# Global attention: the product with the values in two halves of 256 columns, one behind the score matmuls of each head

## The reference

```
xn = layernorm(x)
q, k, v = split(xn @ w_qkv.T)        # 16 heads of 16, q and k rotated (rope)
scores = einsum('blhd,bmhd->bhlm', q, k) / 4
attn = softmax(scores)
s = einsum('bhlm,bmhd->blhd', attn, v) @ w_out.T
```

## Time and profile before

| | us |
|---|---|
| median of 3 runs | 2440.17 (2438.77 to 2447.61) |
| the profiled execution | 2444.06 |
| its span, first to last instruction | 2442.3 |
| global attention within it | about 190 to 888 |

### The profile page before, as it was taken

The page is one execution under the profiler, slowest core; times in us unless marked ns, Lnnn a source line. Parts: engine busy times, 40 slices in busy tenths (PEclk is TensorE's granted clock), DMA queues, the critical chain, the costliest instruction groups (busy, mean ns, idle before and its releaser), DMA issues. The chain is left out here.

```text
span 2442.3 us, 40512 instructions
## 1 busy us (share of the span) xinstructions
PE 2274.1 (93%) x12576; PEld 1315.1 (54%) x12576; DVE 1623.6 (66%) x3777; ACT 1371.3 (56%) x2570; POOL 597.0 (24%) x482
## 2 busy tenths in 40 slices
PE   7969999999999978999999999899999999999868
PEld 4533333333333336666666667567567666666534
DVE  5678999999999926565665556556556556556326
ACT  2216777777777756565555456456456546556321
POOL 4411200000000025333233333233233233323000
PEclk9968999999999989999999999999999999999989
DMA  4584212211112010000000000000100000000016
GB/s 144 182 249 132 57 43 60 61 52 55 50 52 61 27 46 1 1 1 1 0 0 0 0 0 26 1 1 9 35 1 1 0 0 0 0 0 0 1 35 186
DMA packets 71891, 95.83 MB, mean 39 GB/s; under 512 B 13884, under 2 KB 49168, under 8 KB 71696
## 3 DMA queue, kind: packets, MB, share of 16 engines
q1 hardware_dynamic: 71808, 94.78, 12.9%
HBM read 60.67 MB, written 39.49 MB: 41 GB/s over the span
## 5 line engine op out<-in xcount | busy, mean ns | idle before, releaser
L655 DVE TENSOR_REDUCE maxima<-ps_m 128x1 f32<-128x512 f32 x1024 | 635.2, 684 | 63.5 <-PE ps_m L546 59.5
L718 ACT ACTIVATE probs<-ps_st 128x1024 f32<-128x1024 f32 x512 | 496.1, 1021 | 173.1 <-PE ps_st L578 171.5
L546 PE MATMUL ps_m<-k_st,q_st 48*128 48x512 f32 x1024 | 390.7, 468 | 31.8 <-DVE k_st L682 16.2
L1246 ACT ACTIVATE l_probs<-l_probs,l_neg_max 128x256 f32<-128x256 f32 x512 | 254.1, 497 | 222.4 <-DVE l_neg_max L1375 222.4
L578 PE MATMUL ps_st<-q_st,k_st 50*128 50x512 f32 x1024 | 306.5, 426 | 2.7 <-DMA q_st<-max_rows 1.6
L1375 DVE CUSTOM_DVE_ANT_1 l_probs<-ring,l_mask 128x256 f32<-128x256 f32 x384 | 140.1, 421 | 226.9 <-PE ring L1072 226.4
L578 PEld LDWEIGHTS ps_st<-q_st,k_st 50*128 50x128 f32 x1024 | 160.6, 186 | 223.5 <-ACT probs L718 190.3
L1225 ACT COPY p_turned<-ring 128x512 f32<-128x512 f32 x256 | 145.2, 600 | 235.3 <-PE ring L1032 235.3
L591 PE MATMUL ps_o<-probs,v_st 128*32 128x512 f32 x2048 | 274.3, 608 | 0.6 <-ACT probs L718 0.6
L546 PEld LDWEIGHTS ps_m<-k_st,q_st 48*128 48x128 f32 x1024 | 172.0, 190 | 148.2 <-DVE maxima L655 125.4
L992 POOL TENSOR_SCALAR clipped<-sumsq 128x16 f32<-128x16 f32 x64 | 16.1, 252 | 769.3 <-DVE sumsq L1352 769.3
(11 more groups left out here) (150 smaller groups left out, 3808.5 us busy)
## 6 DMA issues: line engine op xcount, KB each, us to landing
qs<-split SPq DMA_DIRECT2D x16, 512.0 KB, 3.5
ks<-split SPq DMA_DIRECT2D x16, 512.0 KB, 5.1
q_st<-qs SPq DMA_DIRECT2D x64, 128.0 KB, 2.6
k_st<-ks SPq DMA_DIRECT2D x64, 128.0 KB, 3.2
o<-o_sb SPq DMA_DIRECT2D x32, 256.0 KB, 2.4
x_in<-in_L_attn_x_dram SPq DMA_DIRECT2D x8, 512.0 KB, 5.9
v<-v_sb SPq DMA_DIRECT2D x16, 256.0 KB, 4.7
q_st<-qs SPq DMA_DIRECT2D x64, 64.0 KB, 2.9
```

What stands on the lines that cost most here:

```text
L546: nc.tensor.matmul(bank(base, use)[:, :], q_st[u][r, qt * P:(qt + 1) * P], k_st[u][r, h * CH:(h + 1) * CH], start=True, stop=True).then_in ...
L655: nc.vector.tensor_reduce(maxima[:, par, side(e), tile + e // 4, e % 2:e % 2 + 1], bank(base, k + e)[:, :], AX_X, ALU.max).then_inc(m_used, 1)
L718: nc.scalar.activation(probs[:, kt % 4, j, :], ps_st[j][:, :], ACT.Exp, scale=float(G_DIM) ** -0.5).then_inc(exp_done, 1)
L1246: nc.scalar.activation(probs[:, head, :], probs[:, head, :], ACT.Exp, bias=neg_max[:, head:head + 1], scale=-1.0, accum_out=total[:, head: ...
```

## The change

`product` gets a parameter `part` and makes only 256 of the 512 columns: part 0 or part 1. In a step the order was s00 m0 s01 m1 s10 m2 s11 m3 and the whole product of the tile before. Now part 1 of the tile before last stands behind head 0's matmuls, and part 0 of the last tile behind head 1's. At a unit's step 0 the unit before is finished: part 1 of its tile 6, then both parts of its tile 7 together. Step 1 has nothing behind head 0. Each part counts `pv_done` up by one, so the three waits on it (ScalarE before an exp and before `copy_o`, GpSimd before `place_v`) count in twos, through `products`. The flag that starts an accumulation stands at tile 0, part 0 alone, and the one that ends it at tile 7, part 1.

```diff
-                def product(n, kt, u):
-
+                def product(n, kt, i, u, part):
+
+                    if u == 0:
+                        pe.wait_ge(v_placed, TILES * i + kt + 1)
                     pe.wait_ge(exp_done, 2 * TILES * n + 2 * kt + 2)
...
+                    q = slice(part * CH // 2, (part + 1) * CH // 2)
...
-                            mm = nc.tensor.matmul(ps_o[r:r + 32, :], v_st[:, kt, 2 * u + j, :],
-                                                  probs[:, kt % 4, j, h * CH:(h + 1) * CH], start=(kt == 0), stop=(kt == TILES - 1))
+                            mm = nc.tensor.matmul(ps_o[r:r + 32, q], v_st[:, kt, 2 * u + j, :],
+                                                  probs[:, kt % 4, j, h * CH + q.start:h * CH + q.stop], start=(kt == 0 and part == 0), stop=(kt == TILES - 1 and part == 1))
                     mm.then_inc(pv_done, 1)
+
+                def last_tile(n, kt, part, i, u, first):
+
+                    if u:
+                        product(n - 1, kt, i, u - 1, part)
+                    elif not first:
+                        product(n - 1, kt, i - 1, NB - 1, part)
+
+                def second_half(i, n, kt, u, first):
+
+                    if kt == 0:
+                        last_tile(n, TILES - 2, 1, i, u, first)
+                    elif kt > 1:
+                        product(n, kt - 2, i, u, 1)
+
+                def first_half(i, n, kt, u, first):
+
+                    if kt == 0:
+                        last_tile(n, TILES - 1, 0, i, u, first)
+                        last_tile(n, TILES - 1, 1, i, u, first)
+                    else:
+                        product(n, kt - 1, i, u, 0)
...
+                            second_half(i, n, kt, u, first)
+                            for h in range(2):
+                                scores(n, kt, u, 1, h, more1)
+                                if m:
+                                    maxima_scores(base, *m[2 + h])
+                            first_half(i, n, kt, u, first)
...
-                                    act.wait_ge(pv_done, TILES * n + kt - 3)
+                                    act.wait_ge(pv_done, products(n, kt - 4))
```

More of the change, by code:

```diff
@@ L389, in global_attention, with products @@
         LOADS = 16 * 8
+        def products(n, kt):
+            return 2 * (TILES * n + kt + 1)
         def side(e):
@@ L525, in body @@
                                 for kt in range(TILES):
-                                    pool.wait_ge(pv_done, TILES * n + kt + 1)
+                                    pool.wait_ge(pv_done, products(n, kt))
                                     place_v(i + 1, kt)
@@ L613, in body @@
                                 turn_maxima(n, kt)
[L615 to L635, removed]
+                            for h in range(2):
+                                if kt == TURN:
+                                    if m and h == 0:
+                                        maxima_scores(base, *m[0])
+                                        maxima_scores(base, *m[1])
+                                    scores(n, kt, u, 0, h, more1)
+                                else:
+                                    scores(n, kt, u, 0, h, more1)
+                                    if m:
+                                        maxima_scores(base, *m[h])
@@ L636, in body @@
+                            second_half(i, n, kt, u, first)
+                            for h in range(2):
+                                scores(n, kt, u, 1, h, more1)
+                                if m:
+                                    maxima_scores(base, *m[2 + h])
+                            first_half(i, n, kt, u, first)
                         if last and u == NB - 1:
-                            product(n, TILES - 1, u)
+                            product(n, TILES - 2, i, u, 1)
@@ L639, in _ @@
+                            product(n, TILES - 1, i, u, 0)
+                            product(n, TILES - 1, i, u, 1)
                 for half in range(2):
@@ L703, in copy_o @@
                 def copy_o(n, i, u):
-                    act.wait_ge(pv_done, TILES * (n + 1))
+                    act.wait_ge(pv_done, products(n, TILES - 1))
                     if not isinstance(i, int) or 2 * i + u // 2:
@@ L716, in body @@
                                 if not isinstance(n, int) or TILES * n + kt >= 4:
-                                    act.wait_ge(pv_done, TILES * n + kt - 3)
+                                    act.wait_ge(pv_done, products(n, kt - 4))
                                 nc.scalar.activation(probs[:, kt % 4, j, :], ps_st[j][:, :], ACT.Exp,
                                                      scale=float(G_DIM) ** -0.5).then_inc(exp_done, 1)
+                                if (kt, j) == (0, 1):
+                                    if u:
+                                        copy_o(n - 1, i, u - 1)
+                                    elif not first:
+                                        copy_o(n - 1, i - 1, NB - 1)
                             if kt == TURN - 1 and (not last or u + 1 < NB):
                                 take_rows(n + 1, i if u + 1 < NB else i + 1, (u + 1) % NB)
[L722 to L726, removed]
                     if last:
```

## The result

| | us |
|---|---|
| before, median of 18 runs | 2440.86 |
| changed, median of 18 runs | 2459.59 |
| ratio of the runs | 1.0068, 95% interval 1.0052 to 1.0083 |
| profiled execution, changed | 2455.66 (span 2453.8); before 2444.06 |

The change is slower, by 0.7%; faster by 1.1% was forecast. The ratio leaves out the one disturbed run of each kernel. The other 17 runs of the changed kernel lie further apart than those before: the shortest took 2442.88 us at a mean granted clock of 0.969, the longest 2469.93 at 0.955.

What follows compares the result with a forecast made beforehand. It took a TensorE-VectorE loop over three banks, 2.71 us a step, as the bound. Units falling from 21.87 to 20.91 us gave 28.8, net 25.7 less: 2418.4 for the profiled execution, 2414 as median, range 2404 to 2437.

Steps and rivals of the forecast that it cites:

- What bounds the step: Global attention: a loop between TensorE and VectorE sets the 2.71 us step; afterwards TensorE's own work bounds it at 2.47.
- The half product: TensorE's product of 256 columns: 0.57 us to the next scores, where a whole one takes 1.00.
- (a): Rival, chance 0.17: switches between score and product layouts cost 0.03 to 0.06 us more per half product; 2428 to 2443 us.
- (b): Rival, chance 0.08: the second pass's weight load is bare, 0.11 us for each half product; slower, 2468 us.
- (c): Rival, chance 0.05: layout switches are partly free and VectorE bounds the step at 2.40 us; 2401 us.
- Step 1: Second step of a unit: no half product behind head 0, so TensorE meets the old wait; 2.28 us.
- Step 6: Step with the transposed maxima: ScalarE's copy starts 0.53 us behind the transpose, scores at 0.93; 3.38 us, before 2.91.
- The end of the attention: The 12 steps without maxima go from 2.21 to 2.47 us each, losing 3.1; other terms there +0.7 and -0.7.
- the sum: Whole kernel: 28.8 us gained in 30 units, plus 0.7, minus 3.1 and 0.7 at the end; net 25.7 less.
- Step 0: First step of a unit: one more half product without another switch, +0.43 us; 2.90 us.
- All on time: Maxima matmuls in the new step: the reductions they need end at 1.22, 1.82 and 2.42 us, so none waits.
- The other stages stand behind barriers and move by nothing: Everything outside the global attention: no change in time, 0 us in the forecast.

Runs made afterwards that it cites:

- the kernel without the branch: The changed kernel with TensorE's hardware loop over the iterations written out, nothing else changed; median 2424.18 us, ratio 0.9949 to the kernel before.

## Why the prediction was wrong

- **What bounds the step** was right: the loop over m0's reduction, m3 and the whole product. Its parts, and the bound that follows it, TensorE's own work at 2.47, came out at 2.46.
- **The half product** was right at 0.57. Rivals (a), (b) and (c) fall: the changes between the two layouts cost what the rows said, and the second pass's weights hide. The rule of the Trainium skill weighed above ("TensorE: Matmul & The Clock Gate", section "The mechanism") would have put the second pass 0.35 behind the first, by the prediction's own sign; it is 0.24 behind, so the rule doesn't hold for these loads.
- **Step 1** was right, 2.28 forecast and measured. **Step 6** took 3.27 and not 3.38: the scores came 0.84 and not 0.93 behind the transpose, since the copy, 0.24 long, started at 0.46 and not at 0.53. **The end of the attention**, units 30 and 31, lost 3.2 us in the kernel without the branch, for 3.1 net in the sum.
- **Step 0** was wrong. "All on time" tested each maxima matmul against the reduction three uses back, and left out that the code counts the banks anew in each unit. 0.41 in each of 31 units is 12.7 us; with the banks in turn a unit was 0.42 shorter, and the median 14. With this term the sum of 25.7 us would have been 13, a little more with the shorter step 6, and the kernel without a branch gained 15.3 in its group of runs, and 14.9 in the attention of its profile.
- **The step that decided** is the sentence that ended the sum: "The other stages stand behind barriers and move by nothing", with the last line's "the sequencer between blocks" as the only mention of TensorE's instruction stream. I priced the product's extra instructions as streaming and weight loads, weighed a cost for each one as it executes and dropped it, and gave no price to how many of them the loop then holds. That number is what cost: 524 instructions more an iteration, 29.5 us in the profile, 14.2 of it five waits for instructions and 15 that went with the clock that fell behind them. The slower rival I had named, (b), was another mechanism; its 28 us are near the size by chance. The evidence was at hand: the page counts the packets of the instruction queue, and the trace before shows none from 370 to 800 us, inside the loop, which says that the loop is held, and asks up to which size.
- The signs: net, -25.7 was forecast; +12.7 for the banks and +29.5 for the branches make +16.5. Measured in the profiled executions +11.6, in the medians +18.7, with a spread that follows the clock.

Left open: exactly which length between 1699 and 1763 is the limit, why it is there, and what else it depends on (where the loop begins in a block was not varied); and why the clock stays down for 3.4 us behind one stall and for 20.5 behind the next of nearly equal length.

## What to carry to other kernels

When an edit adds instructions inside a hardware loop, count the instructions of one iteration on that engine, and look in the profile whether the instruction queue is silent while the loop runs. If it is, the loop is held, and growing it can cost far more than the instructions themselves; write the loop out, or stay below the size. The silence says nothing of how much room is left: the loop of 1699 was as silent as that of 1251. Spreading a long operation between its producers gained a tenth of a step here (2.71 to 2.46), where two engines hand buffers to and fro; when you do so, follow every buffer's index across the wrap, because a shortened step meets waits that the long one had hidden.

## What the runs showed of the hardware

- TensorE looped over up to 1699 instructions without a single instruction fetch from 370 to 800 us, and over 1763 with 39 packets of 16 KB in 430 us and a wait of 3.0 to 3.5 us at each backward branch. In the loop of 1775 the wait ended 1.6 to 1.8 us after a packet of the instruction queue had landed, five times of five. In a straight line, 21 to 32 packets in the same stretch cost no wait.
- A stall of 2.5 to 3.5 us in an engine otherwise fully busy was enough, 10 times of 10, for the granted clock to fall from 2.4 to 1.2 GHz behind it, for 3.4 to 23.9 us.
- A float32 product of 256 columns in four column groups, of two passes, takes 0.57 us between score matmuls where one of 512 takes 1.00; two halves back to back cost 0.05 a unit more than one whole.
